# First rows of x in four transfers, DVE's small operations with two tensor operands, and new orders ahead of the tile loop

## The reference

```python
x = x + tanh(g_xattn[0]) * expert_forward(layernorm(x), fside, ctx)       # int8 linear, silu, int8 linear, per batch
x = x + tanh(g_ffn[0])   * bitlinear_ffn(layernorm(x), gate_w, gate_b, val_w, val_b, out_w, out_b)
x = x + tanh(g_xattn[1]) * (layernorm(x) @ softmax(q k^T) of ctx)          # per batch, 512 x 512 weights
x = x + tanh(g_ffn[1])   * top2_moe(layernorm(x), router_w, down_w, up_w)

def smooth_quant_linear(x, w):          # used twice in expert_forward
    s = max(sqrt(max(amax_x, EPS) / max(amax_w, EPS)), EPS)      # per column
    xs, ws = x / s, w * s
    x_scale = max(max(abs(xs), axis=-1), EPS) / 127              # per row
    w_scale = max(max(abs(ws), axis=-1), EPS) / 127
    return round(xs / x_scale) @ round(ws / w_scale).T * x_scale * w_scale.T
```

## Time and profile before

| | us |
|---|---|
| median of three runs | 468.16 |
| lowest and highest | 467.05 and 469.64 |
| the profiled execution, its own time | 470.15 |
| its span, first to last instruction | 468.4 |

### The profile page before, as it was taken

How to read it: one execution, slowest core, us unless ns; L and a number is a source line. 1 busy time by engine, 2 the same in 40 slices (tenths; PEclk the granted TensorE clock), 3 DMA queues, 4 the chain that set the end, 5 groups by cost and what they waited for, 6 DMA issues and landing times.

```text
span 468.4 us, 7366 instructions
## 1 busy us (share of the span) xinstructions
PE 419.6 (90%) x2183; PEld 245.0 (52%) x2183; DVE 380.8 (81%) x955; ACT 351.1 (75%) x574; POOL 221.6 (47%) x343
## 2 busy tenths in 40 slices
PE   4747879988988987789999999999999999999986
PEld 3736756746745543345455545545545554554563
DVE  3787687989987889377898898889889889888853
ACT  1397798876799989857887787778788778777532
POOL 3276761688796764644343333333424333441220
PEclk9957998999999999999999999999999999999999
DMA  8999668553474701511221331231223123122101
GB/s 303 388 343 302 125 228 177 198 162 68 73 244 90 228 10 23 91 23 33 47 49 42 68 60 42 63 75 38 54 68 46 46 67 60 47 65 67 45 25 45
DMA packets 84936, 49.53 MB, mean 106 GB/s; under 512 B 70936, under 2 KB 73496, under 8 KB 83872
## 3 DMA queue, kind: packets, MB, share of 16 engines
q1 hardware_dynamic: 84896, 49.06, 39.9%
HBM read 28.33 MB, written 4.19 MB: 69 GB/s over the span
## 4 chain that ended last, share of the span: by engine, by line
PE 63%; DVE 10%; ACT 7%; DMA 6%; POOL 6%; issue 5%; SPq 2%; ACTq 0%; DVEq 0%; POOLq 0%
PE p_out L1895 11%; PE p_out L1807 11%; PE p_val L1800 11%; PE p_gate L1800 11%; PE p_tr L1782 3%; DMA att_t<-in_L_ffn_val_w 3%; PE p_out L1829 3%; PE p_out L1855 3%; DMA att_t<-in_L_ffn_gate_w 2%; PE p_tr L1685 2%; ACT val_t L1268 2%; POOL w_slots L529 2%; DVE h_max L775 1%; ACT o_q L1285 1%; PE p_val L1751 1%
## 5 line engine op out<-in xcount | busy, mean ns | idle before, releaser
L1800 PE MATMUL p_gate<-gate_t,q_room 128*128 128x512 fp8e4 x256 | 65.7, 379 | 2.5 <-ACT p_gate L1400 2.5
L1800 PE MATMUL p_val<-val_t,q_room 128*128 128x512 fp8e4 x256 | 65.7, 379 | 0.2 <-ACT p_val L1410 0.2
L1807 PE MATMUL p_out<-att_t,qT_room 128*128 128x512 f32 x120 | 55.4, 603 | 0.9 <-ACT qT_room L1230 0.9
L1895 PE MATMUL p_out<-out_t,ws_f 128*128 128x512 fp8e4 x240 | 54.4, 379 | 1.5 <-DMA ws_f<-ws_f 1.5
L597 POOL TENSOR_TENSOR rstd<-mv,ln_eps 128x1 f32<-128x1 f32 x48 | 9.2, 192 | 94.2 <-DVE mv L866 87.1
L1400 ACT ACTIVATE p_gate<-w_slots,seed_scale 128x512 f32<-128x512 f32 x64 | 43.6, 684 | 11.2 <-POOL seed_scale L618 9.8
L1385 ACT ACTIVATE ctx_sb<-p_gate,bcol 128x512 f32<-128x512 f32 x64 | 43.8, 684 | 9.8 <-issue 4.5
L895 DVE TENSOR_TENSOR act_f<-p_val,ctx_sb 128x512 f32<-128x512 f32 x64 | 44.1, 689 | 6.8 <-PE p_val L1800 5.4
L897 DVE TENSOR_REDUCE mu<-act_f 128x1 f32<-128x512 f32 x64 | 43.9, 686 | 2.2
L1410 ACT ACTIVATE p_val<-w_in,seed_scale 128x512 f32<-128x512 f32 x64 | 43.6, 682 | 0.0
L1800 PEld LDWEIGHTS p_gate<-gate_t,q_room 128*128 128x128 f16 x256 | 24.9, 98 | 31.5 <-issue 8.6
(11 more groups left out here) (242 smaller groups left out, 988.8 us busy)
## 6 DMA issues: line engine op xcount, KB each, us to landing
att_t<-in_L_ffn_out_w SPq DMA_DIRECT2D x6, 1024.0 KB, 5.0
w_in<-in_fside_BxS2xS SPq DMA_DIRECT2D x4, 1024.0 KB, 6.9
att_t<-in_L_ffn_gate_w SPq DMA_DIRECT2D x4, 1024.0 KB, 13.0
att_t<-in_L_ffn_val_w SPq DMA_DIRECT2D x4, 1024.0 KB, 9.4
out_dram<-x_all SPq DMA_DIRECT2D x15, 256.0 KB, 2.3
x_all<-in_x SPq DMA_DIRECT2D x2, 1024.0 KB, 11.2
x_all<-in_x SPq DMA_DIRECT2D x1, 2048.0 KB, 17.3
ctx_sb<-in_ctx SPq DMA_DIRECT2D x4, 512.0 KB, 6.2
```

What stands on the lines that cost most here:

```text
L1800: last = nc.tensor.matmul(bank[:, c % 2, :], x_t[n % 2][:, k * P:(k + 1) * P], w_t[m][:, k, cols], start=False, stop=k == KD - 1, skip_gro ...
L1807: last = nc.tensor.matmul(p_out[:, 0, :], lt_c[:, k * P:(k + 1) * P], att_t[:, bass.ds((n // T) * (KD * S) + k * S, S)], start=k == 0, sto ...
L1895: last = nc.tensor.matmul(p_out[:, 0, :], p_t[:, k * P:(k + 1) * P], w_t[2][:, k, :], start=k == 0, stop=k == KH - 1)
```

## The change

It has four parts.

1. The first batch's rows of x are loaded in four transfers of 128 rows, each with its semaphore, in place of one of 512. `h_statistics(0)` waits for each in turn. The other loads on SP are put in another order: the small weights (`small_loads`, nine transfers) and x of batch 1 now stand ahead of x of batches 2 and 3; `fside_load(1)` stands between the val chunks.
2. DVE's small operations in `ratio`, `smooth` and `row_scales` become `scalar_tensor_tensor` with a second tensor operand: the same tensor again, or the new constant step_share, which POOL writes at the start.
3. `silu_loaded` moves on ACT from behind `b_gate(1, 2)` to the very start.
4. The calls ahead of the loop are in another order on all five engines.

The diff, cut to its core (the orders are shown as places below it):

```diff
+                def first_x_load():
+                    for t in range(T):
+                        sp.dma_start(xs[:, 0, t], xv[:, 0, t]).then_inc(first_x_loaded[t], 16)
...
-                x_load(0, 0)
+                first_x_load()
                 fside_load(0)
                 w_load(0, 0)
-                w_load(0, 2)
                 w_load(0, 3)
                 w_load(0, 1)
+                w_load(0, 2)
+                x_load(1, 1)
+                small_loads()
                 x_load(2, slice(2, NB))
-                x_load(1, 1)
                 val_load(0)
+                val_load(1)
+                fside_load(1)
+                val_load(3)
                 val_load(2)
...
                 def h_statistics(b):
-                    dve.wait_ge(x_loaded[min(b, 2)], 16)
+                    if b > 0:
+                        dve.wait_ge(x_loaded[min(b, 2) - 1], 16)
                     need(dve, a_rstd, b)
                     for t in range(T):
+                        if b == 0:
+                            dve.wait_ge(first_x_loaded[t], 16)
...
-                    link(nc.vector.tensor_scalar(cm[z][:, 0:2, 0:k], src[:, :, 0:k], QUANT_EPS, None, ALU.max))
+                    link(nc.vector.scalar_tensor_tensor(cm[z][:, 0:2, 0:k], src[:, :, 0:k], QUANT_EPS, src[:, :, 0:k], ALU.max, ALU.max))
...
-                    link(nc.vector.tensor_scalar(cm[z][:, 5, 0:k], cm[z][:, 5, 0:k], QUANT_EPS, None, ALU.max))
+                    link(nc.vector.scalar_tensor_tensor(cm[z][:, 5, 0:k], cm[z][:, 5, 0:k], QUANT_EPS, cm[z][:, 5, 0:k], ALU.max, ALU.max))
...
-                    link(nc.vector.tensor_scalar(scale[z][:, r, :], rowmax[z][:, r, :], QUANT_EPS, 1.0 / (QMAX * STEP), ALU.max, ALU.mult))
+                    link(nc.vector.scalar_tensor_tensor(scale[z][:, r, :], rowmax[z][:, r, :], QUANT_EPS, step_share[:, :], ALU.max, ALU.mult))
...
                 h_statistics(0)
                 column_max(0, 0, 1, 0)
                 column_max(0, 0, 1, 1)
-                w_sum(0, 0)
                 column_max(0, 0, 1, 2)
...
                 smooth(0, 0)
+                w_sum(0, 0)
                 w_sum(0, 2)
                 w_mean(0)
                 h_scaled_act(0)
+                h_statistics(1)
                 row_scales(0, 0, 0)
-                h_statistics(1)
+                row_scales(0, 0, 1)
+                h_statistics(2)
+                h_statistics(3)
                 w_sum(1, 0)
...
                 clock_raised(3)
+                clock_raised(2)
+                clock_raised(1)
                 columns(0, 0, 1, 0)
                 columns(0, 0, 1, 1)
                 columns(0, 0, 1, 2)
                 columns(0, 0, 1, 3)
-                clock_raised(2)
+                clock_raised(0)
+                clock_raised(7)
                 columns(0, 0, 0, 0)
```

More of the change, by code:

```diff
@@ L259, in flamingo_gated_kernel @@
         chunk_loaded = [sem(f"chunk_loaded{c}") for c in range(4)]
-        x_loaded = [sem(f"x_loaded{n}") for n in range(3)]
+        first_x_loaded = [sem(f"first_x_loaded{t}") for t in range(T)]
+        x_loaded = [sem(f"x_loaded{n}") for n in range(1, 3)]
         fside_loaded = sem("fside_loaded")
@@ L647, in _ @@
                 h_reciprocal_deviation(2)
+                h_normalise(2)
+                h_reciprocal_deviation(3)
                 w_round(4)
-                h_normalise(2)
                 w_round(5)
+                root(0, 1)
                 w_round(7)
-                root(0, 1)
                 h_hidden(0, 0)
@@ L658, in _ @@
                 root(1, 0)
+                o_scaled_act(0)
                 t_normalise(0, 0)
                 t_normalise(0, 1)
+                root(0, 2)
                 scaled_weights(1, 0)
-                o_scaled_act(0)
-                root(0, 2)
                 t_normalise(0, 2)
+                h_hidden(1, 0)
                 t_normalise(0, 3)
-                h_hidden(1, 0)
                 h_hidden(1, 1)
@@ L672, in _ @@
                 h_hidden(1, 3)
-                o_add(0, 2)
+                h_normalise(3)
+                root(1, 1)
                 t_normalise(1, 0)
                 t_normalise(1, 1)
-                root(1, 1)
-                o_add(0, 3)
-                h_reciprocal_deviation(3)
-                h_normalise(3)
                 o_scaled_act(1)
+                scaled_weights(1, 1)
                 t_normalise(1, 2)
                 t_normalise(1, 3)
-                scaled_weights(1, 1)
+                o_add(0, 2)
+                o_add(0, 3)
                 root(0, 3)
@@ L693, in _ @@
                 o_add(1, 1)
+                h_hidden(2, 2)
+                h_hidden(2, 3)
                 t_normalise(2, 0)
                 t_normalise(2, 1)
-                h_hidden(2, 2)
-                h_hidden(2, 3)
+                root(1, 2)
                 w_round(11)
-                root(1, 2)
-                o_scaled_act(2)
+                q_root(1)
                 t_normalise(2, 2)
                 t_normalise(2, 3)
-                q_root(1)
+                o_scaled_act(2)
                 scaled_weights(1, 2)
@@ L1072, in _ @@
                 h_scaled_act(1)
+                w_sum(2, 0)
                 h_dequantise(0, 2)
@@ L1109, in _ @@
                 o_dequantise(0, 1)
+                o_context_max(1)
+                row_scales(0, 2, 1)
+                o_dequantise(0, 2)
+                o_dequantise(0, 3)
                 t_maximum(1, 0)
                 t_maximum(1, 1)
-                o_dequantise(0, 2)
-                o_dequantise(0, 3)
-                t_reciprocal(1, 0)
                 column_max(1, 1, 0, 0)
@@ L1117, in _ @@
                 ratio(1, 1)
-                row_scales(0, 2, 1)
+                column_max(0, 3, 1, 0)
+                column_max(0, 3, 1, 1)
                 smooth(1, 1)
-                column_max(0, 3, 1, 0)
+                t_reciprocal(1, 0)
+                column_max(0, 3, 1, 2)
+                q_statistics(0)
+                column_max(0, 3, 1, 3)
+                w_sum(2, 2)
                 t_maximum(1, 2)
-                w_sum(2, 2)
                 t_maximum(1, 3)
-                column_max(0, 3, 1, 1)
-                column_max(0, 3, 1, 2)
-                column_max(0, 3, 1, 3)
-                t_reciprocal(1, 2)
                 column_max(0, 3, 0, 0)
                 column_max(0, 3, 0, 1)
+                t_reciprocal(1, 2)
                 column_max(0, 3, 0, 2)
@@ L1144, in _ @@
                 row_scales(0, 3, 0)
+                o_dequantise(1, 0)
+                row_scales(0, 3, 1)
+                o_dequantise(1, 1)
                 t_maximum(2, 0)
                 t_maximum(2, 1)
-                o_dequantise(1, 0)
-                o_dequantise(1, 1)
-                row_scales(0, 3, 1)
-                t_reciprocal(2, 0)
                 o_context_max(2)
@@ L1153, in _ @@
                 o_dequantise(1, 3)
+                t_reciprocal(2, 0)
                 column_max(1, 2, 0, 0)
@@ L1183, in _ @@
                 column_max(1, 3, 0, 1)
+                t_reciprocal(3, 0)
                 ratio(1, 3)
@@ L1535, in _ @@
                 t_transposed(2, 3)
-                q_norm(1)
+                h_silu(3, 0)
                 t_context(3)
+                rounded(1, 2, 0)
                 h_silu(3, 1)
-                rounded(1, 2, 0)
                 rounded(1, 2, 1)
@@ L2066, in _ @@
                 b_chunk(0, 3)
+                t_transpose(3, 0)
                 rows(1, 3)
```

300 lines of the change are left out of this document (145 added, 155 removed).

## The result

| | before | changed |
|---|---|---|
| median, us (14 runs each, side by side) | 468.74 | 470.72 |
| lowest and highest | 466.18 and 470.57 | 468.64 and 473.06 |
| ratio of the two, 95% interval | | 1.0055 (1.0033 to 1.0076) |
| span of the profiled execution | 468.4 | 469.7 |

The change makes the kernel 0.55% slower. The forecast was 1.5 us faster; the result is 2.0 us slower. In all that follows, a ratio is to the kernel before, run beside it on the same chip, with its 95% interval.

The account below looks back on a forecast made before the run. PE bounds the loop from tile 2, so only tile 2's start can move. Gains of 1.0 us up to 120 us and 0.5 behind sum to 1.5, taking the median from 468.16 to 466.7; range 462.8 to 470.8.

Parts of the forecast that it names:

- What bounds the kernel; the loop: From tile 2 on PE bounds the loop; those 259.2 us stay, and only the start of tile 2 can change.
- Start: To 25 us: statistics 1.85 us earlier, rows(0, 0) about 19.4, mean 25.1; bounds 1.9 earlier to 1.4 later.
- 25 to 60: DVE's list of 32.2 us ends smooth(0, 1) at 57.3, 2.4 us earlier; ACT's lead is 3.8 us.
- The small operations: DVE's small operations in the new form lose their delays: value 0.4 us, bounds 0 and 3.3.
- rival 2: The new form still waits for POOL; three waits of 0.55 us cost 1.65: 468.3, no change, chance 0.13.
- 60 to 120: t_maximum(1, 0) at 104.2, row_scales(1, 1, 0) at 118.1; lead between 0 and 1.9, taken as 1.0 us.
- Rival 1: The lead of 60 us, 3.5 to 3.8 us, is kept and reaches the loop: 464.2, chance 0.30.
- 120 to 209: h_hidden(2, 2) about 140.7, o_scaled_act(2) at 150.8, ws_o 0.5 us earlier through to tile 0's output: 0.5 gained.
- Rival 3: At POOL's batch 2, o_scaled_act(2) starts 2.9 us later if t_reciprocal follows the copy by over 1.0: 471.1, chance 0.15.

Follow-up runs that it names:

- the experiment on `w_sum(0, 0)`: Changed kernel with the step as a multiplying reduction (floor left out) and ctx_load(3) early, plus w_sum(0, 0) back between fside's column maxima: ratio 0.9974.
- the forms alone: Kernel before with only the small operations in the three-operand form (scalar_tensor_tensor), all orders as before: ratio 1.0008 (0.9978 to 1.0037).
- one operand: Changed kernel with row_scales' step as a multiplying reduction of pairs (maximum, share), leaving out the 1e-6 floor: ratio 1.0012 (0.9979 to 1.0045).

## Why the prediction was wrong, point by point

- **What bounds the kernel; the loop** unchanged: right.
- **Start.** Mis-sized. Statistics 1.4 earlier (forecast 1.85), but `rows(0, 0)` at 21.3 in place of 19.4 and the mean at 26.7 in place of 25.1. What the working missed here: I moved x's issue without asking what is issued behind it. Three more issues on SP are 1.34 us for fside, and PE waits for fside. By the experiment on `w_sum(0, 0)` the later mean cost nothing that shows in the time.
- **25 to 60.** The sum of DVE's list was right within 0.2 us. Its gain of 2.4 was set against an execution in which smooth(0,1) came at 59.5; over seven traces of the old orders it came at 57.8 in the mean. The true gain is none.
- **The small operations.** Valued at 0.4 saved; the forms alone saved nothing that shows (1.0008), and the mechanism of rival 2 is there in full. Its price was three new waits of 0.55, 1.65 us. There are six waits, 4.0 us in all, and with one operand the time falls by 0.43%, which is about 2 us.
- **60 to 120.** The places were right: `t_maximum(1, 0)` at 105.39 (forecast 104.2, before 101.78), `row_scales(1, 1, 0)` at 118.2 (forecast 118.1). But the lead that was to shrink from 2.4 to 1.0 was hardly there: 0.6 at smooth(0,1) and 0.25 at smooth(0,3), where I had 1.0. Rival 1, that a lead of 3.5 to 3.8 is kept, falls with it.
- **120 to 209.** This is the step that failed. `h_hidden(2, 2)` at 140.4 and `o_scaled_act(2)` at 151.7 came near the forecast (140.7 and 150.8), but the stage, which I took at 0.5 gained, lost 1.5 in the profiled execution (99.0 us from smooth(0,3) to the last product of tile 2, in place of 97.5). The runs show two terms that the sum doesn't have. The wait for `ctx_load(3)`, issued 20 us later on SP, was never weighed: put back, it gives 0.50% (2.3 us). And the waits of the step, which the sum takes as gone, stayed, as rival 2 has it: without them 0.43% comes back, over all stages. `t_query_key(2)` behind a rounding that waits for DVE wasn't weighed either, but it isn't a cause of the loss: putting it back costs 0.5 to 0.6% more.
- **Rival 3**, slower by POOL at batch 2, forecast 471.1 for what became 470.72. The number was near by luck. Its condition, `t_reciprocal(2, 2)` over 1.0 us after the copy, didn't come true: the copy was at 150.19 and the reciprocal at 150.32. `o_scaled_act(2)` did come 2.2 later than before, 1.3 of it because the copy was later, but ws_o came only 0.35 later, and the chain of waits goes over the context and not over this operation.

## What to carry to other kernels

When calls move on a queue, follow every load on it, also those that no wait of the trace points at: one context load issued 20 us later cost 0.50%, about as much as all the waits of the step together (0.43%), and the trace of before showed it issued 28 us ahead of its use. In these runs a small `scalar_tensor_tensor` with two tensors in SBUF waited for POOL just as `tensor_scalar` with one did, and a reduction didn't. If an order is planned on waits being gone, show first that they are gone. And a lead should be set against several executions: here the start varies by 3 us between traces of the same early orders, more than the change was worth.

## What was not expected of the hardware

- A `scalar_tensor_tensor` of 128x4 whose second tensor is a constant took 0.55 to 1.18 us beside POOL's tensor_tensor and tensor_scalar, 0.16 otherwise; a reciprocal of 128x4 between them took 0.178 us each time, and the reduction of pairs 0.161.
- The granted clock fell after short gaps of PE (2.0 us at 10.3, 2.3 us at 137.1) in some executions and not in others of nearly the same program. At the start it fell in 7 of 13 traces of the new early orders and in none of 7 of the old ones; in the 7 smooth(0,1) came at 59.0 in the mean, in the other 6 at 57.1. That this gap comes from the late fside is argued from its rows. Against it: in the two traces with the late fside and the old early orders PE waited longer for it (4.8 and 5.0 us at 10.1 and 10.3), after 8 products of `clock_raised` in place of 24, and the clock stayed at full. Loading fside first was tried once and kept the clock at full there, but brought no time.
